# A ring of ten weight slots with low parts in place, and the first norm's centring and variance as two rounded products each

## The reference

```python
def _layernorm(x, eps=1e-05):
    m = jnp.mean(x, axis=-1, keepdims=True)
    v = jnp.var(x, axis=-1, keepdims=True)
    return (x - m) / jnp.sqrt(v + eps)

# x [4096, 128], adj [4096, 4096], W1 [128, 16], W2 [16, 128, 128], b [16, 128], W [128, 128], B [128]
node = x @ W1
hw = jnp.einsum('nc,kcf->nkf', x, W2)
x0 = jnp.einsum('nk,nkf->nf', node, hw)
x1 = _layernorm(x + relu(adj @ x0 + node @ b))

sens = jnp.exp(-(1.0 / adj - 1.0) ** 2 / (2.0 * 0.5 * 0.5))
weights = jnp.where(adj < 1.0, sens, 0.0)
out = _layernorm(x1 + weights @ (x1 @ W + B))
```

## Time and profile before

| | |
|---|---|
| median of 3 runs | 579.78 us (579.68 to 581.64) |
| profiled execution, its own time | 579.95 us |
| its span, first to last instruction | 577.8 us |
| mean granted TensorE clock | 0.989 |
| PE busy | 561.4 us (97%) |
| DVE busy | 491.1 us (85%) |
| ACT busy | 507.7 us (88%) |
| DMA | 142.24 MB, mean 246 GB/s |

### The profile page before, as it was taken

One profiled execution on the slowest core, in us unless ns is written; L12 is line 12 of the kernel. 1 busy time (PEld: TensorE's weight loads), 2 busy tenths in 40 slices (PEclk: granted clock), 3 DMA queues, 4 the chain that ended last, 5 costly groups with the idle time before them and its releaser, 6 DMA issues.

```text
span 577.8 us, 5251 instructions
## 1 busy us (share of the span) xinstructions
PE 561.4 (97%) x1798; PEld 331.6 (57%) x1798; DVE 491.1 (85%) x542; ACT 507.7 (88%) x464; POOL 82.9 (14%) x74
## 2 busy tenths in 40 slices
PE   9999999999899999999999999999999999889976
PEld 8888888456555655565556555655555565444434
DVE  6777768999879989998999899989998999499742
ACT  5788878799649999989998999899989998999975
POOL 2889999000000000000000000000000000000000
PEclk9999999999899999999999999999999999979999
DMA  5980000689788888888788978887888884435002
GB/s 183 416 353 19 21 0 0 253 339 361 302 304 313 321 295 309 297 325 305 287 319 322 334 276 331 326 300 297 309 314 311 304 301 146 150 145 214 18 36 91
DMA packets 23129, 142.24 MB, mean 246 GB/s; under 512 B 2720, under 2 KB 3136, under 8 KB 6720
## 3 DMA queue, kind: packets, MB, share of 16 engines
q1 hardware_dynamic: 22960, 141.66, 65.3%
q10 hardware_dynamic: 144, 0.26, 0.1%
HBM read 139.81 MB, written 2.10 MB: 246 GB/s over the span
## 4 chain that ended last, share of the span: by engine, by line
PE 78%; ACT 11%; DVE 6%; issue 3%; DMA 2%; SPq 0%; POOL 0%; DVEq 0%; ACTq 0%; POOLq 0%
PE l_ps L444 29%; PE acc_ps L411 12%; PE hw_ps L374 5%; PE hw_ps L380 5%; PE hw_ps L377 5%; PE acc_ps L400 5%; PE acc_ps L402 5%; PE acc_ps L401 5%; ACT wt_pair L565 3%; ACT wt_pair L570 3%; ACT wt_pair L582 3%; DVE wt_pair L721 2%; DMA row_in<-adjT_dram 2%; PE var_ps L428 1%; PE acc_ps L352 1%
## 5 line engine op out<-in xcount | busy, mean ns | idle before, releaser
L444 PE MATMUL l_ps<-wt_pair,msg 128*128 128x512 f32 x504 | 228.1, 597 | 0.0
L444 PEld LDWEIGHTS l_ps<-wt_pair,msg 128*128 128x128 f32 x504 | 96.2, 192 | 111.8 <-issue 110.1
L715 DVE SCALAR_TENSOR_TENSOR wt_pair<-wt_pair 128x2048 f32<-128x2048 f32 x64 | 146.1, 2283 | 0.0
L565 ACT ACTIVATE wt_pair<-wt_pair 128x4096 f32<-128x4096 f32 (+1 forms) x39 | 116.9, 2997 | 8.7 <-DVE wt_pair L715 8.7
L570 ACT ACTIVATE wt_pair<-wt_pair 128x4096 f32<-128x4096 f32 (+1 forms) x39 | 117.3, 3008 | 1.2
L411 PE MATMUL acc_ps<-row_in,x 128*128 128x512 f32 x208 | 93.2, 592 | 0.0
L582 ACT ACTIVATE wt_pair<-wt_pair 128x4096 f32<-128x4096 f32 (+1 forms) x21 | 62.3, 2968 | 31.6 <-DVE wt_pair L721 31.6
L552 ACT ACTIVATE prods<-hw_ps,node 128x128 f32<-128x128 f32 x256 | 73.2, 374 | 17.1 <-PE hw_ps L380 15.6
L708 DVE TENSOR_TENSOR adj_lo<-row_in,adj_hi 128x2048 fp32r<-128x2048 f32 x38 | 87.1, 2292 | 1.3
L721 DVE SCALAR_TENSOR_TENSOR wt_pair<-wt_pair 128x4096 f32<-128x4096 f32 (+1 forms) x21 | 75.7, 3603 | 3.1 <-ACT wt_pair L570 3.1
L675 DVE SCALAR_TENSOR_TENSOR part_acc<-hw_ps,node,part_acc 128x128 f32<-128x128 f32 x224 | 60.7, 343 | 19.3 <-PE hw_ps L380 19.3
(11 more groups left out here) (74 smaller groups left out, 423.7 us busy)
## 6 DMA issues: line engine op xcount, KB each, us to landing
row_in<-adjT_dram SPq DMA_DIRECT2D x64, 1024.0 KB, 6.9
wt_pair<-adjT_dram SPq DMA_DIRECT2D x64, 1024.0 KB, 4.8
x_in<-xT_dram SPq DMA_DIRECT2D x8, 256.0 KB, 3.9
x_row<-xT_dram SPq DMA_DIRECT2D x8, 256.0 KB, 5.9
outT_dram<-sumT SPq DMA_DIRECT2D x7, 256.0 KB, 2.0
W_in<-W_dram SPq DMA_DIRECT2D x3, 256.0 KB, 4.2
W_in<-W_dram ACTq DMA_DIRECT2D x1, 256.0 KB, 3.7
B_sb<-B_dram SPq DMA_DIRECT2D x1, 256.0 KB, 4.1
```

Source lines behind the costliest of these rows:

```text
L444: mm = pe.matmul(l1_ps[:, t % L1_BANKS, :], msg[:, c % 2, k, :], wt[t % WT_RING][:, k, :], start=(k == 0), stop=(k == CH - 1))
L565: act.activation(w, w, ACT.Ln, bias=TINY).then_inc(ln_made, 1)
L715: dve.scalar_tensor_tensor(out=w, in0=w, scalar=1.0, in1=w, op0=ALU.is_lt, op1=ALU.mult).then_inc(mask_made, 1)
```

## The change

- **Rings.** `ROW_RING` goes from 4 to 5, `WT_RING` from 8 to 10, with four late slots loaded at steps 2, 4, 7 and 9. The low part of a split row tile is written over the tile itself (`row_lo` lies on `row_in`), so a row slot is reloaded only when the PE has used the tile.
- **Order of the weights.** Pairs are made two steps earlier (`step = m + COL_LAG - 6`), and reach up to tile 59; only the last four tiles are made singly, in the steps of the new `LAST_...` tuples. The parity of pairs squared on DVE and on ACT is exchanged.
- **First norm.** `centre` and `variance` become two `float32r` products each, of a high and a low part. DVE makes `y_hi`, `y_lo` in `residual` and `sq_lo` in the new `remainder_of_square`; ACT takes the square twice, as `sq` and rounded as `sq_hi`.
- Tile 12 (row 1, g = 4) is no longer split. `x_row` has one buffer. B is held once and read by broadcast.

```diff
-ROW_RING = 4
-WT_RING = 8
-LATE_SLOTS = 2
+ROW_RING = 5
+WT_RING = 10
+LATE_SLOTS = 4
...
-SPLIT_FIRST = (3, 5, 7)
+SPLIT_FIRST = ((3, 5, 7), (1, 3, 5, 7))
...
-LAST_MASKS = (63, 64, 65, 66, 67, 69, 70, 71)
-LAST_STEPS = (64, 65, 66, 67, 68, 70, 71, 72)
-LAST_SQUARES = (65, 67, 68, 70, 71, 73, 74, 75)
-LAST_WEIGHTS = (65, 66, 67, 68, 70, 71, 72, 73)
+LAST_MASKS = (65, 66, 67, 68)
+LAST_STEPS = (66, 67, 68, 69)
+LAST_SQUARES = (67, 68, 69, 70)
+LAST_WEIGHTS = (67, 68, 69, 70)
 LAST_PAIR = 64 - len(LAST_STEPS)
-LATE_AT = (6, 10)
+LATE_AT = (2, 4, 7, 9)
...
         if in_pair(m):
-            return (m - FIRST_PAIR) % 4 < 2
+            return (m - FIRST_PAIR) % 4 >= 2
...
-            step = m + COL_LAG - 4
+            step = m + COL_LAG - 6
...
-                if before >= 0 and is_split(before):
-                    sp.wait_ge(adj_lo_made, split_tiles.index(before) + 1)
-                elif before >= 0:
+                if before >= 0:
                     sp.wait_ge(row_tile_done, before + 1)
...
             def centre(r):
-                pe.wait_ge(y_made, r + 1)
                 if r == 0:
-                    pe.wait_ge(centre_w_filled, 2)
-                pe.matmul(yc_ps[:, :], centre_w[:, :], y[:, :], start=True, stop=True).then_inc(yc_made, 1)
+                    pe.wait_ge(rounded_w_made, 2)
+                pe.wait_ge(y_lo_made, r + 1)
+                pe.matmul(yc_ps[:, :], centre_r[:, :], y_hi[:, :], start=True, stop=False)
+                pe.matmul(yc_ps[:, :], centre_r[:, :], y_lo[:, :], start=False, stop=True).then_inc(yc_made, 1)
...
             def variance(r):
-                pe.wait_ge(sq_made, r + 1)
+                pe.wait_ge(sq_lo_made, r + 1)
                 at_least(pe, msg_copied, r)
-                pe.matmul(var_ps[:, :], mean_w[:, :], sq[:, 0, :], start=True, stop=True).then_inc(var_made, 1)
+                pe.matmul(var_ps[:, :], mean_r[:, :], sq_hi[:, :], start=True, stop=False)
+                pe.matmul(var_ps[:, :], mean_r[:, :], sq_lo[:, :], start=False, stop=True).then_inc(var_made, 1)
...
             def square(r):
...
-                act.activation(sq[:, 0, :], yc_ps[:, :], ACT.Square).then_inc(sq_made, 1)
+                act.activation(sq[0][:, :], yc_ps[:, :], ACT.Square).then_inc(sq_made, 1)
+                act.activation(sq_hi[:, :], yc_ps[:, :], ACT.Square).then_inc(sq_hi_made, 1)
...
             def residual(r):
...
+                dve.wait_ge(y_made, r + 1)
+                dve.tensor_copy(y_hi[:, :], y[:, :]).then_inc(y_hi_made, 1)
+                dve.wait_ge(y_hi_made, r + 1)
+                dve.tensor_tensor(y_lo[:, :], y[:, :], y_hi[:, :], ALU.subtract).then_inc(y_lo_made, 1)
+
+            def remainder_of_square(r):
+                dve.wait_ge(sq_made, r + 1)
+                dve.wait_ge(sq_hi_made, r + 1)
+                dve.tensor_tensor(sq_lo[:, :], sq[0][:, :], sq_hi[:, :], ALU.subtract).then_inc(sq_lo_made, 1)
...
+                if i == TILES + 3:
+                    copy_messages(NB - 1)
                 if 1 <= r <= NB and i == row_added_step(r - 1):
                     add_row(r - 1)
                 if j >= 3:
                     finish(j - 3)
+                if i == TILES:
+                    remainder_of_square(NB - 1)
                 for m in dve_squares_at.get(i, []):
                     take_square(m)
                 for t in masks_at.get(i, []):
                     mask(t)
-                if i == TILES + 2:
-                    copy_messages(NB - 1)
+                if g == 1 and 1 <= r < NB:
+                    remainder_of_square(r - 1)
```

More of the change, by code:

```diff
@@ L74, in gnn_kernel @@
     TILES = NB * NB
-    assert D == P and xT.shape[1] == N and HALF == 2 and NB == WT_RING
+    assert D == P and xT.shape[1] == N and HALF == 2 and NB <= WT_RING
     def in_pair(m):
@@ L125, in gnn_kernel @@
         exps_at.setdefault(step, []).append(m)
-    lo_order = [g for g in SPLIT if g in SPLIT_FIRST] + [g for g in SPLIT if g not in SPLIT_FIRST]
+    lo_order = list(dict.fromkeys([i % NB for i in split_tiles]))
     LAST = TILES - 1
@@ L161, in gnn_kernel @@
         sumT = sb("sumT", [P, N])
-        row_in = [sb(f"row_in_{s}", [P, CH, BW]) for s in range(ROW_RING)]
+        with ExitStack() as whole:
+            row_in = [sb(f"row_in_{s}", [P, CH, BW], F32, whole) for s in range(ROW_RING)]
+        row_lo = [sb(f"row_lo_{s}", [P, CH, BW], F32R) for s in range(ROW_RING)]
         wt_pair = [sb(f"wt_pair_{s}", [P, 2, CH, BW]) for s in range((WT_RING - LATE_SLOTS) // 2)]
-        x_row = sb("x_row", [P, 2, BW])
+        x_row = sb("x_row", [P, BW])
         W_sb = sb("W_sb", [P, P])
-        W1_sb = sb("W1_sb", [P, K])
-        W1T_sb = sb("W1T_sb", [K, P])
-        b0_sb = sb("b0_sb", [K, P])
         W1b = sb("W1b", [P, P])
-        B_sb = sb("B_sb", [P, CH, P])
+        B_sb = sb("B_sb", [P, P])
         mean_w = sb("mean_w", [P, P])
@@ L183, in gnn_kernel @@
             part_acc = sb("part_acc", [P, HALF, P], F32, first)
+            W1_sb = sb("W1_sb", [P, K], F32, first)
+            W1T_sb = sb("W1T_sb", [K, P], F32, first)
+            b0_sb = sb("b0_sb", [K, P], F32, first)
         if SPLIT:
             adj_hi = [sb(f"adj_hi_{s}", [P, CH, BW], F32R) for s in range(2)]
-            adj_lo = [sb(f"adj_lo_{s}", [P, CH, BW], F32R) for s in range(2)]
         wt_pair += [sb(f"wt_pair_{s}", [P, 2, CH, BW]) for s in range((WT_RING - LATE_SLOTS) // 2, WT_RING // 2)]
@@ L190, in gnn_kernel @@
         y = sb("y", [P, BW])
-        sq = sb("sq", [P, 2, BW])
-        rstd = sb("rstd", [P, 2, BW])
+        with ExitStack() as first_norm:
+            y_hi = sb("y_hi", [P, BW], F32R, first_norm)
+            y_lo = sb("y_lo", [P, BW], F32R, first_norm)
+            sq_hi, sq_lo = y_hi, y_lo
+        odd_sq = sb("odd_sq", [P, BW])
+        odd_rstd = sb("odd_rstd", [P, BW])
+        sq = [sb("sq", [P, BW]), odd_sq]
+        rstd = [sb("rstd", [P, BW]), odd_rstd]
+        mean_r = sb("mean_r", [P, P], F32R)
+        centre_r = sb("centre_r", [P, P], F32R)
         x1T = y
@@ L217, in gnn_kernel @@
         x_in_sem = [sem(f"x_in_{s}") for s in range(2)]
-        x_row_in = [sem(f"x_row_in_{s}") for s in range(2)]
+        x_row_in = sem("x_row_in")
         row_tile_in = [sem(f"row_tile_in_{s}") for s in range(ROW_RING)]
@@ L242, in gnn_kernel @@
         y_made = sem("y_made")
+        y_hi_made = sem("y_hi_made")
+        y_lo_made = sem("y_lo_made")
+        sq_hi_made = sem("sq_hi_made")
+        sq_lo_made = sem("sq_lo_made")
+        rounded_w_made = sem("rounded_w_made")
         yc_made = sem("yc_made")
@@ L295, in load_x_row @@
             def load_x_row(r):
[L296 to L297 removed]
+                at_least(sp, y_made, r)
+                sp.dma_start(x_row[:, :], block_of(xT, r)).then_inc(x_row_in, 16)
             def load_x(g):
@@ L322, in _ @@
             for i in range(TILES + COL_LAG):
-                if i % NB == 1 and i // NB + 1 < NB:
-                    load_x_row(i // NB + 1)
+                if i % NB == 1 and 1 <= i // NB < NB:
+                    load_x_row(i // NB)
                 if i + ROW_RING < TILES:
@@ L594, in inverse_root @@
                 at_least(act, x1_made, r)
-                act.activation(rstd[:, 0, :], var_ps[:, :], ACT.Ln, bias=EPS).then_inc(ln_var_made, 1)
+                act.activation(rstd[0][:, :], var_ps[:, :], ACT.Ln, bias=EPS).then_inc(ln_var_made, 1)
                 act.wait_ge(ln_var_made, r + 1)
-                act.activation(rstd[:, 0, :], rstd[:, 0, :], ACT.Exp, scale=-0.5).then_inc(rstd_made, 1)
+                act.activation(rstd[0][:, :], rstd[0][:, :], ACT.Exp, scale=-0.5).then_inc(rstd_made, 1)
             def square2(u):
@@ L601, in square2 @@
                 at_least(act, var2_made, u - 1)
-                act.activation(sq[:, u % 2, 0:width(u)], yc2_ps[u], ACT.Square).then_inc(sq2_made, 1)
+                act.activation(sq[u % 2][:, 0:width(u)], yc2_ps[u], ACT.Square).then_inc(sq2_made, 1)
             def inverse_root2(u):
-                root = rstd[:, u % 2, 0:width(u)]
+                root = rstd[u % 2][:, 0:width(u)]
                 act.wait_ge(var2_made, u + 1)
```

31 lines of the change are left out of this document (18 added, 13 removed).

## The result

| | before | after |
|---|---|---|
| median, same chip | 581.39 us (579.51 to 583.01, 10 runs) | 585.56 us (583.15 to 588.10, 10 runs) |
| ratio after / before | | 1.0085 [1.0068, 1.0101] |
| profiled execution, its own time | 579.95 us | 585.0 us |
| its span | 577.8 us | 583.2 us |

The change made the kernel slower by 0.85%; the forecast was no change. 585.56 lies above the range.

The account below looks back on a forecast made before the run. The PE was taken as the bound, busy 561.4 of 577.8 us. Terms -4.8 - 1.9 + 5.9 = -0.8 gave span 577.0, own time 579.1, likeliest 579.0 us; range 574.5 to 583.5.

Parts of the forecast that it names:

- First norm, steady rows: Rows 2 to 7: split centring and variance products save the PE 0.80 us per row, -4.8 us if DVE and ACT follow.
- nothing else moves: Steady rows: shifted pairs and exchanged parity leave each value of g the same kinds of instructions; no further effect.
- Until the first column tile: Start of the kernel: shorter wait before tile 13 and no clock fall after it, -1.9 us; with a fall 0.
- that rival: Early row tiles come late because the PE frees slots: 1 to 3 us of wait plus half clock, 581 to 584; chance 0.10.
- The tail: From row 7's node bias: PE idle 14.7 us before centre2(0), restart +1.4; 88.4 against 82.48 us, +5.9 us.
- The tail isn't held: Rival, tail: ACT enters earlier or runs ahead; 5 us earlier give 574, ten 569; chance 0.13.
- DVE falls behind in the steady rows: Rival, at remainder_of_square: the PE's variance waits in six rows; 1.5 us beyond the room per row give 588; chance 0.15.
- Two steps more of lead help nobody while the PE never waits for weights: Making weight pairs two steps earlier was claimed to bring no gain; no size given.

Follow-up runs that it names:

- Messages early: Kernel after, with DVE's copy_messages moved to step g = 4, between square and mask; 583.31 us, 1.0038 of the kernel before.
- the float32 run: Kernel after, with centring and variance of the first norm back to one float32 product each; 584.31 us, 1.0056 of the kernel before.
- both: Kernel after, with copy_messages in step g = 4 and the steps of the last four single tiles reordered; 569.27 us, 0.9801 of the kernel before.
- its float32 form: "both", with centring and variance of the first norm as one float32 product each; 568.53 us, 0.9799 of the kernel before.
- best version: "both" with pair 58's square on DVE, masks of 62 and 63 late, row 7's inverse root early; float32 564.86 us (0.9740), rounded 566.11 us (0.9742).
- the new order of the last tiles: Kernel after, with only the steps, DVE squares and exponentials of the last four single tiles moved; 570.34 us, 0.9826 of the kernel before.
- the lead taken back: "both", with pairs, their parity and the last four tiles two steps later, ten-slot ring kept; 581.35 us, 1.0004 of the kernel before.
- pair 58 squared on DVE: "both", with the square of pair 58 on DVE instead of ACT and last-tile steps adjusted; 569.97 us, 0.9831 of the kernel before.
- the inverse root early: "pair 58 squared on DVE", with row 7's inverse root before pair 56's exponential, its scaling one step earlier, mask 6 one step later; 571.30 us, 0.9846.

## Why the prediction was wrong

**First norm, steady rows (-4.8, measured -0.12): the step that failed.** The forecast put it so: "there is no stall", on a walk that compared DVE's instructions with the PE's at the centring, the variance and the splits. All of these held: no wait before a centring from row 2 on, one of 0.34 before a variance (row 2 only), DVE's wait at g = 7 at 1.60 (forecast 1.7), the square at g = 4 at 365.72 - 331.55 = 34.2 after the node bias (forecast 33.8, counted from 0.16 us later). What the walk left out was `copy_messages`, two instructions behind that square, whose consumer is the column tile of g = 5. That deadline lies at 41.3 of the row; DVE meets it at 41.4. Before, there were 1.1 us of room (copy ended at 40.8, tile at 42.0 of the row); the deadline then came 0.7 us earlier and the copy 0.55 later, which is just too much. Against the forecast's 54.24 the cost is 2.76 us in row 2 (waits of 1.94 and 0.34, the rest after them) and 0.39 in each of the other five: 4.7 in all, the whole gain. "Messages early" gives 4.2 back with that one edit, which shows the cause.

Not all of it is the norm's. The forecast's "nothing else moves" failed too: the float32 run shows that the rest of the change costs 1.0 us in these rows, nearly all in row 2, where the copy is late in float32 as well. The norm by itself brought 1.1 us there, not 4.8.

Behind it stands a second reason that the forecast's sum didn't have at all: its terms add, and here they don't. The 4.2 us won bring the PE into the tail earlier, where ACT is late, and the tail takes 3.0 of them (messages early), 2.4 (both), 4.6 (both against its float32 form), 2.8 (best version). In the last two the rounded tail also has one more square on ACT and three more instructions on DVE; the share of these isn't separated. A gain of about 4 us in the rows is worth -0.7 to +1.8 us at the end. So the rounding would have brought about 1 us at most without the missed wait too (-0.7 in "both", 1.2 in the best version).

**Until the first column tile (-1.9, measured -1.45).** At the column tile itself it is -1.33: the twelve matmuls of tile 13 took 4.32 us before and take 2.81, and they start 0.18 later. Right in place: the wait before tile 13 is 1.54 (forecast about 1.5), the clock stays at 1.00 after it, and the centring waits 0.76 for y_lo (forecast 0.75). From this stretch on neither the PE nor DVE waited for a transfer; that rival is out.

**The tail (+5.9, measured +5.12).** Right step by step: no wait at the variance of row 7, 1.68 before the messages (1.7), 14.57 before `centre2(0)` (14.7), held by the squares as walked. The restart cost 1.6 us, 1.01 for the centring and 0.56 for the column tile behind it, where 1.4 was taken. That this size was hit is luck: in the other runs such a restart cost 2.2 to 3.2. About 1.0 us of the 5.12 belongs to the rounded norm, by the float32 run. "The tail isn't held" is out.

**The rivals.** "DVE falls behind in the steady rows" had the engine and the sign, but its place (`remainder_of_square`) and its price (over 0.65 us in each row) aren't what happened. "Two steps more of lead help nobody while the PE never waits for weights" is right for the rows and wrong for the kernel: by the runs the lead is worth up to 12 us with the new order of the last tiles. In the kernel after it is spent in DVE's waits. What the fifth row slot and the single `x_row` buffer do by themselves no run tells.

**The sum.** -1.45 - 0.12 + 5.12 = +3.6 us lies within the change. The profiled execution adds 1.85 from its first 10 us, which are not part of the change (below). The timed difference, 0.85% of 580, is 4.9 us (3.9 to 5.9), and the medians differ by 4.2; how much of it is that start stays open.

## What to carry to other kernels

For each engine list that gets longer, write down every instruction on it that another engine waits for, with its deadline; a list that is idle at the end of a row can still be late in the middle of it, and the one consumer left out cost the whole gain. In a tail, don't put an instruction that waits for a slow engine ahead of a small one that the critical engine needs: three tuples of step numbers were worth 13 us here, more than all the arithmetic of the change. And before counting a gain in the steady part, ask which engine limits the tail: if it is another one, most of the gain can be given back there.

## What the runs showed of the hardware

- *The start varies between executions of the same instructions.* In after's profiled execution the first float32r products of the kernel go at half speed till 9.2 us, in before's they don't. The PE's timelines, first after, then before:

```profile
6.96 0.63 PE L392 MATMUL hw_ps<-W_hi,x_lo 128*128 128x512 f32 x1
7.39 0.63 PE L395 MATMUL hw_ps<-W_lo,x_hi 128*128 128x512 f32 x1
7.81 0.63 PE L389 MATMUL hw_ps<-W_hi,x_hi 128*128 128x512 f32 x1
```

```profile
6.66 0.40 PE L374 MATMUL hw_ps<-W_hi,x_hi 128*128 128x512 f32 x1
6.89 0.40 PE L377 MATMUL hw_ps<-W_hi,x_lo 128*128 128x512 f32 x1
7.12 0.40 PE L380 MATMUL hw_ps<-W_lo,x_hi 128*128 128x512 f32 x1
```

  One every 0.43 us against one every 0.23. `node_bias(0)` then starts at 128.3 to 128.6 in four profiled executions (after, the lead taken back, both best versions) and at 126.2 to 126.9 in the other eight ("pair 58 squared on DVE" has no usable one). Such a start costs about 2 us, 0.35% of the kernel, not far below what one wants to measure; two traces have to be compared from a node bias on. The five times of the best float32 version fall in two groups, 564.7 to 564.9 and 567.2 to 567.4, and the profiled one with the slow start is in the upper; that the start makes the groups is likely, not shown. The rounded version has the same groups, 563.68 and 566.06 to 566.39; it is about 1.1 us faster in either, as the rows say, and its median is the higher one only because more of its executions fell in the upper group. The windows show a granted clock of 1.00 over these 10 us in both, so it is the spacing that shows it. The Trainium skill (TensorE: Matmul & The Clock Gate, Part 1) says that the gate's window runs free of the kernel and that one kernel therefore starts differently from run to run; the traces agree that it does, but as they show the clock at 1.00 they don't show that the gate is the cause.
- *After an idle time the clock falls.* After 14.57, 13.53, 12.90, 8.32, 5.79 and 3.81 us a centring or variance took 2.07 or 2.08 us instead of 1.02. The eight small matmuls of the messages took 1.16 us after 1.68 and 1.69 of idle time, 1.91 and 1.76 after 2.34, 2.08 after 9.65. After 1.94 and 1.54 the granted clock stayed at 1.00, after 2.17 (before) it was 0.51. Length alone doesn't decide near 2 us: after 2.07 (the lead taken back) it fell to 0.51, after 2.13 (the inverse root early) it stayed at 1.00.
- *A restart costs 1.6 to 3.2 us, and not more after a longer idle time.* Over the product behind the wait and the column tile after it the PE lost 1.6 us after 14.57 us of idle time, 2.8 after 13.53, 2.5 after 12.90, 2.2 after 8.32 and 3.2 after 5.79, against 0.86 and 3.43 at full clock. These are different kernels; no run shows two executions of one.
- *Short waits cost more than they last.* A row of after with a shown wait of 0.15 to 0.19 us is 0.4 us longer than one of "messages early" without it (54.63 against 54.2). From its start to the next tile's start, the column tile behind the wait takes 3.53 us instead of 3.43 (373.01 to 376.54); the rest fits with the overlap of one matmul with the next, which a wait also interrupts, but no run isolates it.
